# A graph network on one core: loads move from SyncE to ScalarE in one stage, and SyncE's steps are written out in two others

## The reference, cut to what matters

```python
h = relu(layernorm(x)); x = x + mean_over_edges(h[src], edge_attr_128)    # layer 0
h = relu(layernorm(x)); x = x + sparse_attention_block(h, src, dst)       # layer 1
h = relu(layernorm(x)); x = x + gated_sum_block(h, src, dst, edge_attr_32)# layer 2
h = relu(layernorm(x)); x = x + mean_per_relation(h[src], edge_type_8)    # layer 3
```

## Time and profile before

| | us |
|---|---|
| median of 3 runs | 6305.19 (6295.0 to 6335.05) |
| profiled execution, its own time | 6339.22 |
| its span, from the first to the last instruction | 6336.6 |
| around the span | 2.6 |
| PE / DVE / POOL / ACT busy | 3965.5 / 3891.3 / 3033.6 / 1969.8 |
| mean granted TensorE clock | 0.809 |

### The profile page before, as it was taken

The page is one execution under the profiler, slowest core; times in us unless marked ns, Lnnn a source line. Parts: engine busy times, 40 slices in busy tenths (PEclk is TensorE's granted clock), DMA queues, the critical chain, the costliest instruction groups (busy, mean ns, idle before and its releaser), DMA issues. The chain is left out here.

```text
span 6336.6 us, 84284 instructions
## 1 busy us (share of the span) xinstructions
PE 3965.5 (63%) x16962; PEld 2615.5 (41%) x16962; DVE 3891.3 (61%) x12524; ACT 1969.8 (31%) x4351; POOL 3033.6 (48%) x2764
## 2 busy tenths in 40 slices
PE   0577733332699974589644457778564777777740
PEld 0355532221377763544444346667321333333320
DVE  7566657774488854644444446666596666666656
ACT  0454522322122221255444432222363222222210
POOL 0656626666666500000355548888402565666630
PEclk9788865555799998999766779998897888888875
DMA  6466646654445546867555557777694111111139
GB/s 216 118 137 141 142 128 192 186 178 141 112 127 139 144 164 206 276 227 228 195 175 176 170 154 131 130 131 130 176 371 160 24 31 32 35 38 38 39 130 376
DMA packets 972277, 957.72 MB, mean 151 GB/s; under 512 B 208975, under 2 KB 659295, under 8 KB 971855
## 3 DMA queue, kind: packets, MB, share of 16 engines
q1 hardware_dynamic: 676703, 615.07, 33.4%
q0 software_dynamic: 131904, 146.31, 11.5%
q10 hardware_dynamic: 163376, 193.25, 8.6%
HBM read 547.91 MB, written 440.47 MB: 156 GB/s over the span
## 5 line engine op out<-in xcount | busy, mean ns | idle before, releaser
L709 POOL DMA_INDIRECT at_first_table<-n_h,n_first_edge x784 | 805.4, 1027 | 1497.3 <-ACT n_h L277 904.2
L2481 PE MATMUL e_m<-e_by_rel,rel_w 128*128 128x512 f32 x1568 | 767.5, 646 | 5.1 <-issue 5.1
L2395 DVE SCALAR_TENSOR_TENSOR e_by_rel<-e_y,e_part_t 128x512 f32<-128x512 f32 x784 | 477.1, 681 | 388.4 <-DMA sum_high_table<-e_res,e_target 320.0
L701 POOL DMA_INDIRECT e_xs<-x_table,e_idx x392 | 377.5, 963 | 435.6 <-DMA e_idx<-idx_table 299.7
L709 POOL DMA_INDIRECT rel_sum_table<-e_res,e_again x392 | 395.6, 1009 | 388.1 <-DMA e_again<-row_tab_table 251.7
L701 POOL DMA_INDIRECT e_x<-x,e_idx x392 | 404.0, 1031 | 337.0 <-DMA e_idx<-idx_table 160.8
L701 POOL DMA_INDIRECT e_hs<-h_table,e_idx x392 | 420.1, 1072 | 221.5 <-issue 116.3
L987 PE MATMUL n_m<-n_mean,n_pick 128*128 128x129 f32 x784 | 204.7, 442 | 453.3 <-DVE n_pick L1052 274.7
L2481 PEld LDWEIGHTS e_m<-e_by_rel,rel_w 128*128 128x128 f32 x1568 | 323.3, 212 | 382.8 <-issue 382.8
L987 PEld LDWEIGHTS n_m<-n_mean,n_pick 128*128 128x128 f32 x784 | 175.6, 329 | 482.3 <-DVE n_pick L1052 290.1
L1955 PE MATMUL n_o<-w_center_cat,n_h2t 128*128 128x128 f32 x784 | 173.3, 390 | 320.5 <-ACT n_h2t L1922 269.0
(11 more groups left out here) (373 smaller groups left out, 10161.4 us busy)
## 6 DMA issues: line engine op xcount, KB each, us to landing
x_table<-n_x ACTq DMA_DIRECT2D x294, 256.0 KB
n_x<-x_table SPq DMA_DIRECT2D x294, 256.0 KB
e_hd<-at_first_table SPq DMA_DIRECT2D x196, 256.0 KB
e_keep<-col_tab_table SPq DMA_DIRECT2D x294, 128.0 KB
mean_runs_table<-e_packed SPq DMA_DIRECT2D x196, 130.0 KB
n_mean<-mean_runs_table SPq DMA_DIRECT2D x392, 65.0 KB
at_first_table<-prep_zero ACTq DMA_DIRECT2D x1, 25088.0 KB
e_edge<-edge128T SPq DMA_DIRECT2D x98, 256.0 KB
```

Of the source, the lines that this page charges most:

```text
L701: pool.indirect_dma_start(out=tile[:, t, :], out_offset=None, in_=table, in_offset=bass.IndirectOffsetOnAxis(ap=idx[:, col + t:col + t + 1 ...
L709: pool.indirect_dma_start(out=table, out_offset=bass.IndirectOffsetOnAxis(ap=idx[:, t:t + 1], axis=0), in_=tile[:, t, :], in_offset=None, ...
L2395: ins = dve.scalar_tensor_tensor(at(by_rel, u - 5)[:, r, :], flat(ps_y), float(r), at(part_t, u - 5)[:, :], ALU.is_equal, ALU.mult)
L2481: ins = pe.matmul(flat(at(ps_m, u - 6)), k.rel_w[:, r, :], at(by_rel, u - 6)[:, r, :], start=(r == 0), stop=(r == RELS - 1))
```

## The change: what it does

- `attention_edges`: SyncE keeps only the chained stores. ScalarE issues the loads of `hd` and `keep` (two steps ahead of its own step, at the end of the step), of `row` (tile n - 28) and of `group_keep`, and one zero store into `rel_sum` in each of its first 98 steps.
- The table of starts holds 2 + 4 values a tile where it held 4 + 4, and the two stages with chained stores read two values for a tile, so two FUSED_REGOPS and two SEQ_ASSERT a tile are gone in each. The other readers of the table read as many values as before, from another column.
- `second_norm_nodes` and `relation_edges`: SyncE's steps are written out with `each_step`; the other engines keep their loops.

```diff
@@ mean_edges, SyncE
-                sp.dma_start(run_rows(scratch["mean_runs"], begins[2 * h], HALVES),
+                sp.dma_start(run_rows(scratch["mean_runs"], begins[h], HALVES),
...
-                    begins = starts_of(nc, k, w, 0, TILES)
+                    begins = starts_of(nc, k, w, 0, HALVES)
@@ attention_edges, SyncE
-            sp.wait_ge(zero_ready, 1)
-            for n in range(STEPS + 6):
-                i = n
-                if i < S:
-                    if i >= 4:
-                        sp.wait_ge(hd_turned, i - 3)
-                    sp.dma_start(at(hd, i)[:, :, :], in_order(scratch["at_first"], i)).then_inc(at(hd_in, i), 16)
-                    if i >= 4:
-                        sp.wait_ge(hdt_ready, i - 3)
-                    sp.dma_start(at(keep, i)[:, :], keep_values_of(scratch, i)).then_inc(at(keep_in, i), 16)
-                if n >= S:
-                    for part in range((n - S) * 3, min((n - S) * 3 + 3, S)):
-                        sp.dma_start(rows_of(scratch["rel_sum"], part), zero[:, :]).then_inc(zeroed, 16)
...
-                w = n - 40
-                if 0 <= w < S:
-                    begins = starts_of(nc, k, w, 0, TILES)
-                    sp.wait_ge(packed_ready, w + 1)
...
+            for w in range(S):
+                begins = starts_of(nc, k, w, 0, HALVES)
+                sp.wait_ge(packed_ready, w + 1)
+                for h in range(HALVES):
+                    if w or h:
+                        sp.wait_ge(placed, (w * HALVES + h) * 16)
+                    sp.dma_start(run_rows(scratch["att_runs"], begins[h], HALVES),
+                                 at(packed, w)[:, HALVES * h:HALVES * h + HALVES, :]).then_inc(placed, 16)
             sp.wait_ge(placed, HALVES * 16 * S)
@@ attention_edges, ScalarE
+            def load_dst(i):
+                if i >= 4:
+                    act.wait_ge(hd_turned, i - 3)
+                act.dma_start(at(hd, i)[:, :, :], in_order(scratch["at_first"], i)).then_inc(at(hd_in, i), 16)
+                if i >= 4:
+                    act.wait_ge(hdt_ready, i - 3)
+                act.dma_start(at(keep, i)[:, :], keep_values_of(scratch, i)).then_inc(at(keep_in, i), 16)
+            load_dst(0)
+            load_dst(1)
...
+                if n + 2 < S:
+                    load_dst(n + 2)
+                j = n - 28
+                if 0 <= j < S:
+                    if j >= 4:
+                        act.wait_ge(pick_ready, j - 3)
+                    act.dma_start(at(row, j)[:, :], row_values_of(scratch, j)).then_inc(at(row_in, j), 16)
...
+                if n < S:
+                    act.dma_start(rows_of(scratch["rel_sum"], n), zero[:, :]).then_inc(zeroed, 16)
+            act.wait_ge(zeroed, S * 16)
@@ second_norm_nodes, SyncE
-            run_steps(sp, body, S, 5)
+            each_step(body, S, 5)
@@ relation_edges, SyncE
-            run_steps(sp, body, S, 13, 20)
+            each_step(body, S, 13)
```

More of the change, by code:

```diff
@@ L330, in __init__ @@
         self.local = tile("local", [P, size.steps, TILES])
-        self.starts = tile("starts", [1, size.steps, 2 * TILES], I32)
+        self.starts = tile("starts", [1, size.steps, HALVES + TILES], I32)
         self.last_start = size.rows
@@ L622, in _ @@
             dve.sem_inc(search_made, 1)
-            dve.tensor_scalar(starts_tab[:, 0:TILES], runs[:, ::P], -1.0, None, ALU.add)
+            dve.tensor_scalar(starts_tab[:, 0:HALVES], runs[:, ::HALF], -1.0, None, ALU.add)
             for h in range(HALVES):
@@ L949, in body @@
                 if live(i, S):
-                    begins = starts_of(nc, k, i, TILES, TILES)
+                    begins = starts_of(nc, k, i, HALVES, TILES)
                     if begun(i - 4):
@@ L1422, in _ @@
         def _(act):
+            def load_dst(i):
[7 more added lines that the diff above has]
+            load_dst(1)
             act.wait_ge(consts_ready, 3)
+            act.wait_ge(zero_ready, 1)
             for n in range(STEPS):
@@ L1467, in _ @@
                     act.activation(decay[:, :], fall[:, :], ACT.Exp).then_inc(decay_ready, 1)
+                if n + 2 < S:
[5 more added lines that the diff above has]
+                    act.dma_start(at(row, j)[:, :], row_values_of(scratch, j)).then_inc(at(row_in, j), 16)
+                g, rest = divmod(n - 4, GROUP)
+                if rest == 0 and 0 <= g < G:
+                    if g >= 2:
+                        act.wait_ge(weight_done, g - 1)
+                    rows = scratch["col_tab"][g * GROUP:(g + 1) * GROUP, 0, :]
+                    act.dma_start(group_keep[g % 2][:, 0:ROWS], rows.unsqueeze(1).broadcast_to([GROUP, HEADS, ROWS])
+                                  ).then_inc(group_keep_in[g % 2], 16)
+                    tails = scratch["col_tab"][g * GROUP + 1:(g + 1) * GROUP, 0, 0:1]
+                    act.dma_start(group_keep[g % 2][0:GH - HEADS, ROWS:ROWS + 1],
+                                  tails.unsqueeze(1).broadcast_to([GROUP - 1, HEADS, 1])
+                                  ).then_inc(group_tail_in[g % 2], 16)
+                if n < S:
+                    act.dma_start(rows_of(scratch["rel_sum"], n), zero[:, :]).then_inc(zeroed, 16)
+            act.wait_ge(zeroed, S * 16)
         @block.tensor
@@ L1631, in body @@
                 if live(i, S):
-                    begins = starts_of(nc, k, i, TILES, HALVES)
+                    begins = starts_of(nc, k, i, HALVES, HALVES)
                     if begun(i - 4):
@@ L2619 @@
     scratch["mean_runs"] = table("mean_runs", (R + ROWS, RUN_COLS))
-    scratch["starts"] = table("starts", (S, 2 * TILES), I32)
+    scratch["starts"] = table("starts", (S, HALVES + TILES), I32)
     scratch["search"] = table("search", (S * TILES, 2 * P))
```

28 lines of the change are left out of this document (3 added, 25 removed).

## The result

The changed kernel takes **6227.1 us** (median of 4 runs, 6223.1 to 6236.8), the kernel before 6304.4 us; the ratio is 0.988 with a 95% interval of 0.985 to 0.991. The forecast was 6223. Its sum came out, but two of its terms did not: one gave nothing, one gave about three times as much.

What follows compares the result with a forecast made beforehand. No engine binds the whole; SyncE's list binds the attention edge stage's end and mostly the mean edge stage. Terms -58 + 2 - 18 - 8 - 0 = -82 us give 6223 us against the median 6305.2, range 6170 to 6285.

Steps and rivals of the forecast that it cites:

- The pace: End of attention edge stage: 25 tiles take 126 us instead of 157, 0.5 us extra for ten group steps; 31 saved.
- The backlog: End of attention edge stage: 35.6 us from last `e_p` to last store become one tile's way, 9.1 us; 26.5 saved.
- The term of 58 us: End of attention edge stage: saving from leaving SyncE the chained stores alone, pace and backlog together; bounds 49 to 74.
- The loads on ScalarE: Attention edge stage: ScalarE's added issues take 1.9 us a step, mostly covered; 2 us lost in all.
- The cover of 2.3 us: Attention edge stage: time from the end of `hst` to TensorE's `e_hs`, room for ScalarE's added 1.9 us a step.
- rival (c): Attention edge stage: ScalarE's issues cost twice and hold up the loop, 147 us on top, 6370 us; chance 0.06.
- Two starts instead of four: Mean edge stage: up to 0.52 us saved at each of 68 tiles where SyncE did not wait; 18 us taken.
- Second norm written out: Second norm stage: fewer instructions for each load, costed at 0, bounded by 15 us both ways.
- Relation stage written out: Relation stage: GpSimd's 251.7 us wait for `again` is off the path; half of VectorE's 15.7 us saved, 8 us.
- rival (a): Relation stage: GpSimd is a pacer after all, so 50 us go where 8 were taken; 6181 us, chance 0.15.
- Rival (b): Attention edge stage's end stays at about 6.3 us a tile, mean edges gain nothing; only 27 us saved, 6278, chance 0.17.
- rival (d): Whole kernel: the earlier end is given back elsewhere or by longer stalls, time 6305 us; chance 0.07.

Runs made afterwards that it cites:

- e1_only: Kernel before with the new lists of SyncE and ScalarE in the attention edge stage alone, four starts a tile kept: 6307.8 against 6360.7 us, ratio 0.992.
- starts_only: Kernel before with two register loads a tile in place of four in the two stages with chained stores, nothing else: ratio 1.002.
- long groups: Three of the four groups of follow-up runs, each with the kernel before beside it; that kernel took 6361, 6350 and 6363 us there.
- pauses: again_early with gaps in GpSimd's issues, by waits for its own transfers in mean edge, second norm and relation stages: 6239.1 against 6362.7 us, ratio 0.982.
- short group: One of the four groups of follow-up runs, with the kernel before beside it; that kernel took 5732 us there.
- after_b: The changed kernel run once more, unchanged, as the control of a later group: 6276.7 us, ratio to the kernel before 0.988.
- again_early: Changed kernel with `again` of the relation stage loaded one step earlier, straight behind `idx`: 5677.5 against 5732.0 us for the kernel before, ratio 0.989.

## Why the prediction was right, and where it was not

*What bounds the attention edge stage's end.* Right: the backlog and the pace were SyncE's list. The pace was put at 31 us and gave 37.9: the plain step was put at 4.57 us and is 4.35, which is 5 us of it, and of the 5 us kept for group steps some 3 were needed (three steps of 5.2 us and two of 4.7). The backlog was put at 26.5 us and gave 24.2, since the last tile takes 11.4 us and not 9.1. The term of 58 us measured 62 at the end and 58 in the stage. In `e1_only` it is 48 us (35 to 62) of the time.

*The loads on ScalarE.* 1.9 us a step was right, 2 us in all somewhat low (about 4 ahead of the end). The cover of 2.3 us was read from a single tight step where the median is 4.1. So rival (c), which was to decide from 2.3 us a step, falls: at 3.9 us a step it cost 16 us and not 147. Beside ScalarE's issues the two stores of a tile start 2.29 us apart (mean of 98) where it was 2.02. But they start 2.23 us apart in `starts_only`, where ScalarE issues none of these loads, so the difference isn't shown to be ScalarE's. The rule of the Trainium skill, Perfetto Trace Analysis, section "DMA Instruction — HWDGE (DVE, Sync)", that the block which makes the descriptors is locked for one issuer, gets neither support nor contradiction from it.

*Two starts instead of four.* Wrong, 0 instead of 18 us: `starts_only` gives 1.002. The step that failed is that SyncE binds at the 68 tiles where it did not wait. From a tile's second store to the next tile's first it takes 3.85 us before and after (mean of 97), while the wait grew by 31.9 us (54.9 against 23.0) of the 51 that the instructions took. The standstills are part of what does bind this stage in the long groups: `pauses` has 720 us against 730 to 755, and the short group 689 to 695. What binds the rest is open.

*Second norm written out.* Right: 0.

*Relation stage written out.* The step "the large wait is idle time of an engine off the path" failed. It was to give 8 us and gave 25 (13 to 38), half of what rival (a) had for it. (Rival (a) took off the landing of 98 loads where only 42 waits stood; its 50 us were no bound.) GpSimd is the pacer: 10.3 us a step where nothing else disturbs, and the wait for `again` comes on top of it. That VectorE hardly waits for gathers (15.7 us) was no proof, because the standstill held VectorE at the same time as it held `again`. The profile before had the sign: VectorE idle for 388.4 us ahead of `e_by_rel`, 320.0 of them put down to a transfer of another stage.

*The sum.* -58 + 2 - 18 - 8 was forecast. The parts alone gave -48, +12, -25 and +7 us (the positive ones not told from 0), -54 with intervals of 10 to 17 us to each side, and the whole -77 and, in the control, -73; the 20 us between can't be told from nothing. That 6223 was met by 4 us is luck: the 18 us too much and the 17 too little cancel. Rival (b) falls by the 37.9 us of pace, rival (d) by the result.

## What to carry to other kernels

A chain of dependent DMAs deserves a queue whose issuer does nothing else behind the last producer; what can be issued earlier, or by an engine with idle time, should be, and the gain is the pace and the backlog, two terms read apart. A few instructions taken from a queue that then waits for a landing gave nothing here. Where several engines start again within 0.2 us and the profile names a releaser from another stage, look at what a fourth engine did just before: the wait that is then longest may be a consequence and still pace the stage.

## What the runs showed of the hardware that was not expected

In the profiles of before and after and in the traces of two groups, engines stood for 3 to 7 us although what they waited for was done, while GpSimd issued indirect DMAs of 1.0 us each with 0.3 us between them in runs of mostly 14 to 40 us (16 issues, 20.2 us, in the relation stage; one of 8.6 us in `after_b`); they went on some 2 to 3 us after the last issue. In the same stretches SyncE's register instructions took 0.70 us where they take 0.03 to 0.06.

In the short group GpSimd issued in the same way without a gap for 505 us (second norm) and 906 us (relation), and nothing stood: the same changed stages took 526 instead of 681 to 688 us and 1051 to 1055 instead of 1284 to 1296, and the kernel before 5732 instead of 6304 to 6363 us. The 600 us between the spans of `after_b` and `again_early` lie all in the five stages of the table above, in each of which GpSimd issues such DMAs; this is eight times the change studied here. It didn't follow the chip's number, so a kernel of this sort is to be compared with its control in one group, whatever the chip.
